# Four steps of entries spread ahead of the branch, values copied by ScalarE, 19 tiles projected while counting

## The reference, cut to what matters

```
Q, K, V = (proj(Wq, bq), proj(Wk, bk), proj(Wv, bv))     # x @ W.T + b, 16 heads of 16
use_sparse = LAMBDA_MAX * exp(-ALPHA * u_prev) >= 1
idx = prior_indices[:S]                                   # 32 keys for each query, drawn from 0..255
s_scores = einsum('bhsd,bhskd->bhsk', Q, K[:, :, idx]) * scale
s_scores = where(prior_index_mask, s_scores, -inf)
sparse_out = einsum('bhsk,bhskd->bhsd', softmax(s_scores), V[:, :, idx])
out = where(use_sparse, sparse_out, dense_out)
return out @ Wo.T + bo
```

## Time and profile before

| what | value |
|---|---|
| runs | 521.99, 522.18, 524.74 us |
| profiled execution | 521.58 us, span 519.6 us |
| PE busy | 473.9 us, 91% |
| DVE busy | 386.8 us, 74% |
| ACT busy | 257.9 us, 50% |
| POOL busy | 94.7 us, 18% |
| opening, first to last EQ | 9.02 to 41.9 us |
| first maximum of the attention proper | 48.51 us |

### The profile page before, as it was taken

One profiled execution on the slowest core, in us unless ns is written; L12 is line 12 of the kernel. 1 busy time (PEld: TensorE's weight loads), 2 busy tenths in 40 slices (PEclk: granted clock), 3 DMA queues, 4 the chain that ended last, 5 costly groups with the idle time before them and its releaser, 6 DMA issues.

```text
span 519.6 us, 7588 instructions
## 1 busy us (share of the span) xinstructions
PE 473.9 (91%) x2479; PEld 325.5 (63%) x2479; DVE 386.8 (74%) x763; ACT 257.9 (50%) x506; POOL 94.7 (18%) x97
## 2 busy tenths in 40 slices
PE   4998889999999999898999999999999898979982
PEld 2445554444454444346888888888888687968861
DVE  4997889979879999784884788478846783624367
ACT  2016578677877775854462635262635242544300
POOL 3003101111111112000100026002600240456610
PEclk9999999999999999989999999999999989798995
DMA  7900020999300000021132201110201016253266
GB/s 227 234 0 1 1 81 0 343 304 339 108 1 0 1 1 1 0 82 51 54 69 77 88 0 68 55 42 1 82 2 42 21 62 163 67 168 124 94 212 216
DMA packets 24095, 45.25 MB, mean 87 GB/s; under 512 B 7938, under 2 KB 17794, under 8 KB 23778
## 3 DMA queue, kind: packets, MB, share of 16 engines
q1 hardware_dynamic: 21410, 37.46, 23.8%
q0 software_dynamic: 2640, 7.24, 3.9%
HBM read 35.29 MB, written 23.00 MB: 112 GB/s over the span
## 4 chain that ended last, share of the span: by engine, by line
PE 45%; DVE 4%; ACT 1%; DMA 1%; issue 1%; another core or an unknown queue 1%; SPq 0%; ACTq 0%; DVEq 0%
PE psG L1638 6%; PE psG L1640 6%; PE psG L1639 6%; PE psS L1638 5%; PE psS L1640 5%; PE psS L1639 4%; PE psO L1638 2%; PE psO L1640 2%; PE psO L1639 2%; PE psM L1638 1%; PE psM L1640 1%; PE psM L1639 1%; DVE attT L1926 1%; DMA back<-expert_results 1%; PE psM L1738 1%
## 5 line engine op out<-in xcount | busy, mean ns | idle before, releaser
L681 ACT ACTIVATE Pr<-psS 128x512 f32<-128x512 f32 x128 | 69.7, 599 | 40.7 <-PE psS L538 40.2
L758 DVE TENSOR_REDUCE few_Qa<-psG 128x2 fp32r<-128x512 f32 x116 | 74.4, 683 | 12.3 <-PE psG L523 12.3
L766 DVE SCALAR_TENSOR_TENSOR Pr<-Pr,few_W 128x1024 f32<-128x1024 f32 x64 | 79.1, 1242 | 2.8 <-ACT Pr L681 2.6
L521 PE MATMUL psG<-few_KG,QG 128*128 128x512 f32 x116 | 53.1, 498 | 3.3 <-DVE few_Qa L758 3.1
L538 PE MATMUL psS<-few_QAT,few_KP 128*128 128x512 f32 x128 | 49.5, 460 | 4.1 <-ACT Pr L681 2.4
L1878 DVE TENSOR_TENSOR hT_lo<-V,hT_hi 128x512 fp32r<-128x512 f32 x64 | 44.3, 693 | 2.2
L523 PE MATMUL psG<-Mneg,few_identb 128*128 128x512 bf16 x116 | 45.2, 390 | 0.0
L1876 DVE CAST hT_hi<-V 128x512 fp32r<-128x512 f32 x64 | 27.4, 428 | 19.6 <-ACT V L1813 11.2
L386 POOL TENSOR_TENSOR few_Qa<-Qn,few_Qa 128x256 fp32r<-128x256 f32 x16 | 18.4, 1150 | 128.9 <-ACT few_Qa L624 128.9
L538 PEld LDWEIGHTS psS<-few_QAT,few_KP 128*128 128x128 f32 x128 | 21.1, 192 | 30.4 <-issue 26.3
L1860 POOL DMA_INDIRECT expert_results<-block_out,block_rows x31 | 30.1, 972 | 40.6 <-ACT block_out L1794 32.4
(11 more groups left out here) (299 smaller groups left out, 1159.9 us busy)
## 6 DMA issues: line engine op xcount, KB each, us to landing
expert_rows<-blank_dram SPq DMA_DIRECT2D x8, 1548.0 KB, 23.6
block_rows<-expert_rows SPq DMA_DIRECT2D x31, 129.0 KB, 2.1
back<-expert_results SPq DMA_DIRECT2D x6, 512.0 KB, 6.6
staged<-w_dram SPq DMA_DIRECT2D x4, 512.0 KB, 4.5
x1T<-xT_dram SPq DMA_DIRECT2D x4, 512.0 KB, 4.4
staged<-ew_dram SPq DMA_DIRECT2D x4, 512.0 KB, 3.5
few_idxb<-entries_by_query SPq DMA_DIRECT2D x8, 192.0 KB, 6.9
out_dram<-attT SPq DMA_DIRECT2D x6, 256.0 KB, 2.7
```

Of the source, the lines that this page charges most:

```text
L521: nc.tensor.matmul(o, QG[:, (u // 2) % 2, st * P:st * P + P], self.KG[:, u % 2, 2 * p:2 * p + 2, :], start=True, stop=False)
L681: nc.scalar.activation(Pr[:, i % JOBS, 512 * f:512 * f + 512], psS[:, f, :], ACT.Exp, scale=SCALE).then_inc(self.s["s_exp"], 1)
L758: nc.vector.tensor_reduce(self.Qa[:, f % SLOTS, st, 2 * p:2 * p + 2, 48], self.guard_bank(i)[0][:, p, :].rearrange("p (h t) -> p h t", h=2 ...
L766: nc.vector.scalar_tensor_tensor(pr, pr, FMAX, self.W[:, r, :], ALU.min, ALU.mult).then_inc(self.s["s_prob"], 1)
```

## The change

Four things are altered.

1. **Spread.** Steps 0 to 3 are spread instead of 0 and 1, by 64 matmuls and four ACT copies, in the setup, ahead of the branch. `ident16` is made by ACT, not DVE; the constants' DMA is issued one place earlier. PE and ACT branch after this work.
2. **Values.** DVE's add of a key and value tile is now the key half alone. ACT copies the values without a bias (line 629 of the new file), and the value bias is added in *turn*, where the copy to `attT` becomes an ACTIVATE with two new columns of `cols` as bias, which first waits for the load of `cols`.
3. **Tiles.** 19 tiles are projected while counting instead of 16, by new tables; the first count stands ahead of the first projection; *guard_keys* stands ahead of tiles 15 and 16; *mask_keys* and *fill* come before the last two counts. From tile 12 on the tiles use the two banks of `psO` alone.
4. **Counts.** `few_W` is copied in three parts, the last by DVE; both halves are transposed at once (the second into `psS`), then both halves of `Mneg` are made, then tile 19 is projected.

```diff
-SPREAD = 2
-FAR = ((SPREAD, 5), (5, STEPS))
-PROJECT_AT = (((0,), (1,)), ((2,), (3,)), ((4,), (5,)), ((6,), (7, 8)), ((9,), (10,)), ((11,), (12,)), ((13,), (14, 15)),
+SPREAD = 4
+FAR = ((SPREAD, 6), (6, STEPS))
+PROJECT_AT = (((), (0,)), ((1,), (2,)), ((3,), (4,)), ((5,), (6, 7)), ((8,), (9,)), ((10,), (11,)), ((12, 13), (14,)),
...
-LATE_TILES = 4
+TWO_BANKS = 12
+LATE_TILES = 1
...
         def setup_tensor(pe):
             pe.wait_ge(s["greatest"], 1)
             pe.wait_ge(L["cst"], 16)
-            nc.tensor.transpose(psM[0:1, 0, 0:P], flags[:, 0:1], ident).then_inc(s["greatest_full"], 1)
+            nc.tensor.transpose(psG[0:1, 0, 0:P], flags[:, 0:1], ident).then_inc(s["greatest_full"], 1)
+            pe.wait_ge(s["consts_ready"], 1)
+            pe.wait_ge(s["idx_ready"], 1)
+            for i in range(SPREAD):
+                if spread_bank(i) is psG:
+                    pe.wait_ge(s["self_setup"], 6)
...
+                mm.then_inc(s["spread_full"], 1)
...
         def setup_act(act):
+            act.wait_ge(L["cst"], 16)
+            nc.scalar.copy(ident16[:, :], ident).then_inc(s["consts_ready"], 1)
             act.wait_ge(L["u"], 16)
             nc.scalar.activation(lam[:, 1, :], lam[:, 0, :], ACT.Exp, scale=-ALPHA).then_inc(s["lam_exp"], 1)
+            nc.scalar.copy(atts[0].sum16[:, :], sum32).then_inc(s["sums_ready"], 1)
+            for i in range(SPREAD):
+                act.wait_ge(s["spread_full"], i + 1)
+                nc.scalar.copy(atts[0].idxb[:, i, :],
+                               spread_bank(i)[:, :, :].rearrange("p a b -> p (a b)")).then_inc(s["spread_out"], 1)
...
                 for k in range(STEPS):
                     for tt in range(NT):
-                        for n in PROJECT_AT[k][tt]:
-                            yield "project", n
                         if (k, tt) == (STEPS - 1, 0):
                             yield "copy_keys", 0
                             yield "guard_keys", 0
                             yield "split_keys", 0
+                            yield "mask_keys", 0
+                            yield "fill", 0
+                        for n in PROJECT_AT[k][tt]:
+                            yield "project", n
                         yield "count", k * NT + tt
                 yield "counted", 0
-                yield "mask_keys", 0
-                yield "fill", 0
-                late = B * (NT + NQ) - LATE_TILES
                 for half in range(2):
-                    for j in range(LATE_TILES // 2):
-                        yield "project", late + half * LATE_TILES // 2 + j
                     yield "turn_counts", half
+                for n in range(B * (NT + NQ) - LATE_TILES, B * (NT + NQ)):
+                    yield "project", n
...
+                    if what == "project" and not tiles[i][0]:
+                        _, b, tt = tiles[i]
+                        act.wait_ge(self.s["proj_out"], i + 1)
+                        nc.scalar.copy(va[:, b * NT + tt, :, 0:DH],
+                                       self.projected_bank(i)[:, D:2 * D].rearrange("p (h d) -> p h d", d=DH)).then_inc(self.s["v_out"], 1)
                     if what == "counted":
...
+                        act.wait_ge(self.s["eq_used"], STEPS * NT - 1)
+                        nc.scalar.copy(self.W[:, 0, :], psG[:, :, :].rearrange("p a b -> p (a b)")).then_inc(self.s["w_out"], 1)
+                        act.wait_ge(self.s["eq_used"], STEPS * NT)
+                        nc.scalar.copy(self.W[:, 1, 0:512], psS[:, 0, :]).then_inc(self.s["w_out"], 1)
...
                     if what == "turn":
                         b, half = divmod(i, GROUPS // 2)
+                        if i == 0:
+                            act.wait_ge(L["cols"], 16)
...
-                            nc.scalar.copy(attT[:, half, t0:t0 + 512], self.misc_bank("at_out", n)).then_inc(
+                            nc.scalar.activation(attT[:, half, t0:t0 + 512], self.misc_bank("at_out", n), ACT.Identity,
+                                                 bias=cols[:, 20 + half:21 + half]).then_inc(
...
+                    if what == "counted":
+                        dve.wait_ge(self.s["eq_used"], STEPS * NT)
+                        nc.vector.tensor_copy(self.W[:, 1, 512:1024], psS[:, 1, :]).then_inc(self.s["w_out_more"], 1)
...
             sp.dma_start(msk4[:, :], io["msk4"]).then_inc(L["idx"], 16)
+            sp.dma_start(cst[:, :], io["consts"]).then_inc(L["cst"], 16)
             sp.dma_start(lam[:, 0, :], io["u"]).then_inc(L["u"], 16)
-            sp.dma_start(cst[:, :], io["consts"]).then_inc(L["cst"], 16)
```

More of the change, by code:

```diff
@@ L125, in bass_adaln_ffn @@
         attT = sb("attT", [P, KD, N], F32)
-        cols = sb("cols", [P, 20], F32)
+        cols = sb("cols", [P, 22], F32)
         cbias = sb("cbias", [P, B, KD], F32)
@@ L213, in setup_tensor, with spread_bank @@
             pe.wait_ge(L["cst"], 16)
-            nc.tensor.transpose(psM[0:1, 0, 0:P], flags[:, 0:1], ident).then_inc(s["greatest_full"], 1)
+            nc.tensor.transpose(psG[0:1, 0, 0:P], flags[:, 0:1], ident).then_inc(s["greatest_full"], 1)
[4 more added lines that the diff above has]
+                    pe.wait_ge(s["self_setup"], 6)
+                flat = spread_bank(i)[:, :, :].rearrange("p a b -> p (a b)")
+                for qq in range(4):
+                    for j in range(4):
+                        p0 = i * 16 + j * 4 + qq
+                        mm = nc.tensor.matmul(flat[32 * j:32 * j + 32, qq * 256:qq * 256 + 256],
+                                              ident16[:, p0:p0 + 1].to_broadcast([P, 32]),
+                                              idxm[:, :], start=True, stop=True, tile_position=(0, 32 * j))
+                mm.then_inc(s["spread_full"], 1)
+        def spread_bank(i):
+            return (psO, psM, psG, psS)[i]
         def either(eng, run):
@@ L274, in opening, with projected_bank, keys_and_values @@
                             yield "split_keys", 0
+                            yield "mask_keys", 0
+                            yield "fill", 0
+                        for n in PROJECT_AT[k][tt]:
+                            yield "project", n
                         yield "count", k * NT + tt
                 yield "counted", 0
-                yield "mask_keys", 0
-                yield "fill", 0
-                late = B * (NT + NQ) - LATE_TILES
                 for half in range(2):
-                    for j in range(LATE_TILES // 2):
-                        yield "project", late + half * LATE_TILES // 2 + j
                     yield "turn_counts", half
+                for n in range(B * (NT + NQ) - LATE_TILES, B * (NT + NQ)):
+                    yield "project", n
+            def projected_bank(self, n):
+                return psM[:, n % 2, :] if n < TWO_BANKS and n % 4 >= 2 else psO[:, n % 2, :]
+            def keys_and_values(self, n):
+                return sum(not is_q for is_q, _, _ in list(self.projected_tiles())[:n])
             def due(self):
@@ L411, in misc @@
                     return self.misc_bank(name, i)
[L413 to L416, removed]
+                pe.wait_ge(s["sums_ready"], 1)
                 for what, i in self.opening():
[L418 to L423, removed]
-                                                      ident16[:, p0:p0 + 1].to_broadcast([P, 32]),
-                                                      idxm[:, :], start=True, stop=True, tile_position=(0, 32 * j))
-                        mm.then_inc(self.s["bc_full"], 1)
                     if what == "project":
@@ L574, in tensor, with turned @@
                             mm.then_inc(self.s["at_full"], 1)
+            def turned(self, half):
+                return (psS if half else psO)[:, :, :].rearrange("p a b -> p (a b)")
             def turn_keys(self, pe, misc, i):
```

78 lines of the change are left out of this document (34 added, 44 removed).

## The result

The changed kernel takes 543.74 us (543.24 to 543.79, four runs), the kernel before 523.46 (four runs too); the ratio is 1.0388, 95% interval 1.036 to 1.0416, so 20.3 us more. The forecast was 13.3 more and its range ended at 540. The direction and the main mechanism hold; two terms of the sum and one step that stood in no term do not.

What follows compares the result with a forecast made beforehand. VectorE was taken to bound the opening, with TensorE having little to spare. 521.58 us + 12.0 (first maximum at 60.5 instead of 48.51) + 1.7 (bias in the turn) = 535.3, stated as 535.5; range 531.5 to 540.

Steps and rivals of the forecast that it cites:

- Adds that wait, 15.3 us: Counting, tiles 5 to 18: VectorE waits before adds for tiles projected too shortly before, 15.3 us in sum.
- PE is back between 8.9 and 9.7. I take 9.1: Opening: TensorE, after four spreads, flag and branch, is ready for its first count at 9.1 us.
- the 1.0 allowed: Opening, first key tile: 1.0 us of loss at TensorE's slow clock, bounds 0 and 1.7.
- The bias in the turn, +1.7: First turn: ScalarE's first copy waits 2.4 us for `cols`, TensorE's transposes come 1.7 us later; bounds 0 and 2.4.
- The tail, -1.7: From the last EQ's end to the first maximum: 4.9 us instead of 6.6, a gain of 1.7.
- From there the attention runs as a fixed pipeline: From the first maximum on: a shift of the attention's start moves its end by as much.
- The rival with the clock: Counting, 20 to 56 us: TensorE's clock at the half level half of the time, +8, 543.5 us; chance 8%.
- the 535.3 of the sum: Whole kernel, execution like the profiled one: 521.58 + 12.0 + 1.7 = 535.3 us.

Runs made afterwards that it cites:

- the two ratios: Changed kernel with later adds, memsets ahead of the branch and biases loaded early: 0.9945 with GpSimd's subtraction waiting for VectorE's 48th multiplication, 1.001 without.
- the sixteen tiles in their second form: Changed kernel with 16 tiles projected while counting, memsets and biases early, GpSimd's subtraction waiting, count copies first, two late tiles before the turns: 507.44 us, ratio 0.9917.

## Why the prediction was wrong, step by step

- **Adds that wait, 15.3 us: right.** The waits agree within 0.1 to 0.3 us each, the stretch within 0.1, and moving the adds alone gave 12.3 us back.
- **"PE is back between 8.9 and 9.7. I take 9.1": this term failed.** It assumed that the first four EQs are done when TensorE is back, at 0.395 us for every EQ. That price comes from the earlier trace rows, where GpSimd is idle. The change draws the EQs forward by 2.3 us, onto the memsets. The first count came at 11.33, 2.2 late, and took 0.16 more; the first key tile, at the slow clock, lost 1.5 instead of the 1.0 allowed. Together tile 4's add was 2.9 us late (it ended at 23.17 instead of 20.25). The counting added 0.1, the tail did 0.16 better: the first maximum was 2.86 late. The warning was in the earlier trace rows: eight EQs in 3.86 us are 0.6 more than at my price, and it was the first of them (1.07 us from 9.02), which ended 0.3 us behind this memset of the kernel before:

```profile
8.00 1.81 POOL L376 MEMSET few_KP<- 128x2048 f32 x1
```

- **The bias in the turn, +1.7: mechanism right, size 2.35.** The load landed 39.5 us after its issue, as forecast, but everything behind TensorE's transposes moved by nearly the whole wait of 2.78. In four other profiles that load `cols` late the shift grew by 1.4, 2.0, 2.0 and 2.5 there, so 1.7 lies within what executions show.
- **The tail, -1.7: right,** 2.0.
- **"From there the attention runs as a fixed pipeline": wrong at one place.** The order of two instructions 0.05 us apart turned over and cost 2.55 us net, part of it by the clock behind. What made VectorE some 0.4 us later there is open: its reciprocal in front of it starts 0.37 later behind TensorE's transposes, in every variant of the change.
- **The rival with the clock** was named at +8; it is real but small, 1.7 us in some executions. The Trainium skill, "TensorE: Matmul & The Clock Gate", section "A second HAM failure mode: psum-queue depth-cycling", was the reason to name it: it tells of a clock that swings between its two levels where TensorE idles briefly between groups. In the counting of five profiles the clock fell once in three and not at all in two, each time for some 3 of 35 us, where the rival had half of the stretch.

With 2.86, 0.65 and 2.55 added, the 535.3 of the sum become 541.4 for an execution like the profiled one, which took 543.71; the 2.3 that are left stand in the expert layer, and their cause is open.

## What to carry to other kernels

A price that is read where the other engines are idle is no price for the same instruction where they are not. When a change moves instructions forward, list what already runs in the place they move to, on GpSimd above all, and move that out of the way: here four memsets could stand before the branch, where GpSimd was idle. An add that follows its product too closely couples two engines that were both busy; count how many independent instructions stand between, against the time from the last input to the product's end. A turnover in the order of two instructions far behind the change can eat the gain: here it cost 1.7 us, and 3.3 where TensorE's clock fell behind it. One wait fixes the order; the 0.65% between the two ratios is not fully borne out by the traces, and their intervals just part (0.9988 and 0.9991).

## What the hardware showed

- VectorE's 128x1024 f16 comparison and GpSimd's f32 memsets did not run side by side in these rows: the comparison took 0.47 us alone and ended 0.3 us behind the memset beside it (0.86, 1.25, 2.10), and the memsets of 0.95 and 1.81 us took 0.28 longer.
- VectorE's 128x1024 f32 multiplication (1.22 us alone) and GpSimd's subtraction (2.38 alone) take whole turns: 3.16 and 2.38, or 1.22 and 3.40, by a lead of 0.31 or 0.05 us.
- TensorE's first key tile took 3.48 us behind an idle time of 3.36 (granted 0.50 from 12 to 15 us) and 1.98 behind one of 0.53. The length of the gap alone does not decide: with the sixteen tiles in their second form it took 3.65 us behind gaps of 0.71 and 0.97.
- The same opening was granted the full clock throughout the counting in two profiles and for some 3 us only 0.50 in three.
